# Expert routing in two halves of the tokens, with the first product and silu of two tiles computed during the routing

## The chip, the cores and the metric

The kernel runs on one core of one Trainium2 chip. The metric is the device time of one execution in microseconds, and the number quoted is the median of several executions. The profile shows one further execution of the same program: for each engine its instructions with start and duration, and what released it after each idle stretch.

## The reference

A small image and text model of one block. Thirty-two images pass through a Fourier operator of four layers and become 64 tokens of width 64 each; 77 text tokens are appended to each image, so there are 32 * 141 = 4512 tokens. An attention follows, and then a mixture of experts, which is all that the change touches:

```
h = h + ffn(layernorm(h))
logits   = x @ gate_w + gate_b                 # 16 experts
probs    = softmax(logits)
top-2 of probs, divided by their sum           -> dispatch[token, expert], zero elsewhere
h1 = x @ w1[e]; h2 = x @ w2[e]                 # 64 -> 128, for every expert
hidden = silu(h1) * h2
out = sum over e of dispatch[token, e] * (hidden @ w3[e])     # 128 -> 64
```

Every expert is computed for every token, and the shares of the two chosen experts weigh the results. All numbers are float32.

## The kernel before, in words

The program is a chain of blocks with a barrier of all engines between them: the Fourier operator and its head, the attention, and `build_moe` (L1379 on). Every engine's list of instructions is written out by hand, and engines are ordered by semaphores alone; each engine works through its list in order, so an instruction that waits holds all that stand behind it on that engine. SyncE (SP) issues all transfers.

In the expert block the 4512 tokens stand on 96 partitions with 47 tokens each. A tile is 4 such columns, 384 tokens; there are 12 tiles, the last with 288. Each tile has 8 steps, each for a pair of experts, one on partitions 0 to 63 and the other on 64 to 127; so there are 96 steps, s = 8 t + c.

The block begins with the layernorm (DVE and ACT, four chunks), 47 transposes of the tokens (L1486, into `xT`), and 94 small products for the logits (L1494). DVE adds the bias (L1631), subtracts the maximum (L1632, L1633), ACT takes the exponential (L1563), and DVE computes the shares of all 47 columns in a chain of 20 instructions (L1635 to L1652) in which each waits for the one before (`link`). PE transposes the shares (L1499); DVE and ACT copy one half of them each to `dTs` (L1654, L1565). SP stores them to `dT_d` in DRAM with six transfers (L1448), waits until all have landed, and then loads them back, spread over 64 partitions, into `dB` (L1457). One load group n is two transfers and serves four steps; `dB` holds two groups, so group n waits for GpSimd to be done with group n-2.

Then come the steps. For step s:

- PE computes h1 = w1 * xT (L1520), when the product of step s-2 is done;
- ACT takes its silu into `s1` (L1579);
- GpSimd (POOL) computes dx = xT * dB, tokens times share (L1475), into one of three buffers: it may be three steps ahead of PE;
- PE computes h2 = w2 * dx (L1527);
- DVE multiplies silu and h2 into `hid` (L1668).

h1 and h2 take turns in three pairs of PSUM banks, `HP2`. After 8 steps PE sums hid * w3 of the tile in `MA` (L1535, 16 matmul instructions, which the profile counts as 32), ACT copies the sum (L1571), PE folds the halves into `MO` (L1509), one tile late, and DVE adds them to `H` (L1659).

The wait of the main part on PE is of few lines:

```
for c in range(EP):
    s = t * EP + c
    if s >= 2:
        pe.wait_ge(S["prod"], s - 1)
    ...
    pe.wait_ge(S["dx"], s + 1)
    if s >= 1:
        pe.wait_ge(S["silu"], s)
    ...
```

Of the kernel before, what the change touches and what calls it, by code (L numbers as in the profile page):

```python
# [890 lines left out]
ROWS = 96  # L891
PER = TOK // ROWS
# [4 lines left out]
EXPERTS, HID = 16, 128  # L897
# [480 lines left out]
def build_moe(nc, H, out, dT_d, gate, gateb, w12, w3, aconst):  # L1378
# [3 lines left out]
    ALU, ACT, AX = mybir.AluOpType, mybir.ActivationFunctionType, mybir.AxisListType  # L1382
    ctx = ExitStack()
    with ctx:
        sb = lambda name, shape, dt=f32: ctx.enter_context(nc.sbuf_tensor(name, shape, dt))
        sem = lambda name: ctx.enter_context(nc.semaphore(name))
        TILE, EP = 4 * ROWS, EXPERTS // 2
# [3 lines left out]
        def js(t):  # L1391
            return min(4, PER - 4 * t)
# [11 lines left out]
        dB = sb("mdB", [128, 2, EP // 2, TILE])  # L1404
        dx = sb("mdx", [128, 3, TILE])
        s1 = sb("ms1", [128, 2, 2, TILE])
        hid = sb("mhid", [128, EP, 2, TILE])
        acc = sb("macc", [128, 2, TILE])
        stat = sb("mst", [96, 3 * PER + 1])
# [17 lines left out]
        def bank(i):  # L1427
            return HP2[i // 2][:, i % 2, :]
# [6 lines left out]
        @block.sync  # L1435
        def _(sp):
            sp.dma_start(cst[:, :], aconst[0:96]).then_inc(S["par"], 16)
            for e in range(2):
                r = slice(e * 64, e * 64 + 64)
                sp.dma_start(gs[r, :], gate).then_inc(S["par"], 16)  # L1440
                sp.dma_start(w1s[r], w12.rearrange("d (c e) m -> e d c m", e=2)[e]).then_inc(S["par"], 16)
                sp.dma_start(fold[r, :], aconst[0:64, PER + 128 + EXPERTS:PER + 128 + EXPERTS + 64]).then_inc(S["par"], 16)
            sp.dma_start(w3s[:, :, :], w3).then_inc(S["par"], 16)
            sp.dma_start(gb[:, :], gateb.broadcast_to([96, EXPERTS])).then_inc(S["par"], 16)
            sp.wait_ge(S["dte"], 2)
            for g in range(6):
                k = min(8, PER - 8 * g)
                sp.dma_start(dT_d.rearrange("e (j p) -> j e p", p=96)[8 * g:8 * g + k], dTs[0:16 * k, g, :]).then_inc(S["dst"], 16)  # L1448
            sp.wait_ge(S["dst"], 96)
            d_v = dT_d.rearrange("(c e) n -> e c n", e=2)  # L1450
            for n in range(2 * TILES):
                t, c, k = n // 2, n % 2 * 4, js(n // 2) * 96
                if n >= 2:
                    sp.wait_ge(S["dx"], 4 * (n - 1))
                for e in range(2):
                    src = d_v[e, c:c + 4, t * TILE:t * TILE + k].rearrange("(o c) n -> o c n", o=1).broadcast_to([64, 4, k])
                    sp.dma_start(dB[e * 64:e * 64 + 64, n % 2, :, 0:k], src).then_inc(dbs[n % 2], 16)  # L1457
                if n % 2 == 1 and t >= 2:
                    store_tile(sp, t - 2)
            for t in range(TILES - 2, TILES):  # L1460
                store_tile(sp, t)
            sp.wait_ge(S["st"], 16 * TILES)
# [15 lines left out]
        def _(pe):  # L1478
# [14 lines left out]
                    if j < PER:  # L1493
                        last = nc.tensor.matmul(bank(4 + e)[0:96, i * 16:i * 16 + 16], xT[r, j * 96:j * 96 + 96], gs[r, :], start=True, stop=True)  # L1494
            last.then_inc(S["lg"], 1)
            pe.wait_ge(S["rt"], 1)
            for g in range(6):
                k = 16 * min(8, PER - 8 * g)
                last = nc.tensor.matmul(bank(g // 3)[0:k, g % 3 * 96:g % 3 * 96 + 96], disp[:, g * 128:g * 128 + k], ident[:, 0:96], start=True, stop=True, is_transpose=True)  # L1499
                if g % 3 == 2:  # L1500
                    last.then_inc(S["dt"], 1)
            pe.wait_ge(S["dte"], 2)

            def output(t):
                pe.wait_ge(S["accd"], t + 1)
# [6 lines left out]
            for t in range(TILES):  # L1512
                k = js(t) * 96
                for c in range(EP):
                    s = t * EP + c
                    if s >= 2:
                        pe.wait_ge(S["prod"], s - 1)
                    for e in range(2):
                        r = slice(e * 64, e * 64 + 64)
                        last = nc.tensor.matmul(HP2[2 * s % 3][:, e, 0:k], w1s[r, c, 0:HID], xT[r, t * TILE:t * TILE + k], start=True, stop=True)  # L1520
                    last.then_inc(S["h1"], 1)
                    pe.wait_ge(S["dx"], s + 1)
                    if s >= 1:
                        pe.wait_ge(S["silu"], s)
                    for e in range(2):
                        r = slice(e * 64, e * 64 + 64)
                        last = nc.tensor.matmul(HP2[(2 * s + 1) % 3][:, e, 0:k], w1s[r, c, HID:2 * HID], dx[r, s % 3, 0:k], start=True, stop=True)  # L1527
                    last.then_inc(S["h2"], 1)

                if t:  # L1530
                    pe.wait_ge(S["accd"], t)
                for c in range(EP):
                    pe.wait_ge(S["prod"], t * EP + c + 1)
                    for e in range(2):
                        last = nc.tensor.matmul(MA[e * 64:e * 64 + 64, 0:k], w3s[:, 2 * c + e, :], hid[:, c, e, 0:k], start=c == 0, stop=c == EP - 1)  # L1535
                    last.then_inc(S["acc"], 1)
                if t:
                    output(t - 1)
# [3 lines left out]
        def _(act):  # L1542
# [18 lines left out]
            act.wait_ge(S["lgd"], 1)  # L1561
            lg = scr[:, 0:PER * EXPERTS]
            nc.scalar.activation(lg, lg, ACT.Exp).then_inc(S["lgd"], 1)  # L1563
            act.wait_ge(S["dt"], 2)
            nc.scalar.activation(dTs[:, 3:6, :], bank(1)[:, 0:288].rearrange("p (g n) -> p g n", n=96), ACT.Copy).then_inc(S["dte"], 1)  # L1565

            def whole(t):
                act.wait_ge(S["acc"], (t + 1) * EP)
# [4 lines left out]
            for s in range(STEPS):  # L1573
                t, c = s // EP, s % EP
                k = js(t) * 96
                act.wait_ge(S["h1"], s + 1)
                if s >= 2:
                    act.wait_ge(S["prod"], s - 1)
                nc.scalar.activation(s1[:, s % 2, :, 0:k], HP2[2 * s % 3][:, :, 0:k], ACT.Silu).then_inc(S["silu"], 1)  # L1579
                if c == 1 and t:  # L1580
                    whole(t - 1)
            whole(TILES - 1)
# [2 lines left out]
        def _(dve):  # L1585
            chained = [0]

            def link(ins):
                chained[0] += 1
                ins.then_inc(S["chain"], 1)  # L1590
                dve.wait_ge(S["chain"], chained[0])
# [31 lines left out]
            def over_e(x):  # L1623
                return x.rearrange("p (j o) -> p j o", o=1).broadcast_to([ROWS, PER, E_])

            def over_j(x, k=PER):
                return x.rearrange("p (o e) -> p o e", o=1).broadcast_to([ROWS, k, E_])
# [4 lines left out]
            link(nc.vector.tensor_reduce(cols[0], lg, axis=AX.X, op=ALU.max))  # L1632
            nc.vector.tensor_tensor(lg, lg, over_e(cols[0]), ALU.subtract).then_inc(S["lgd"], 1)  # L1633
            dve.wait_ge(S["lgd"], 2)
            link(nc.vector.tensor_reduce(cols[0], lg, axis=AX.X, op=ALU.add))  # L1635
            link(nc.vector.reciprocal(cols[0], cols[0]))
            link(nc.vector.tensor_tensor(pr, lg, over_e(cols[0]), ALU.mult))
            link(nc.vector.tensor_copy(rest, pr))
            for top, one in ((cols[1], one1), (cols[2], one2)):
                link(nc.vector.tensor_reduce(top, rest, axis=AX.X, op=ALU.max))  # L1640
                link(nc.vector.tensor_tensor(hit, rest, over_e(top), ALU.is_equal))  # L1641

                link(nc.vector.scalar_tensor_tensor(idx, hit, -float(E_), over_j(order), ALU.mult, ALU.add))  # L1643
                link(nc.vector.tensor_reduce(cols[3], idx, axis=AX.X, op=ALU.min))
                link(nc.vector.tensor_tensor(one, idx, over_e(cols[3]), ALU.is_equal))
                if one is one1:
                    link(nc.vector.scalar_tensor_tensor(rest, one, -2.0, rest, ALU.mult, ALU.add))
            link(nc.vector.tensor_tensor(cols[1], cols[1], cols[2], ALU.add))
            link(nc.vector.reciprocal(cols[1], cols[1]))
            link(nc.vector.tensor_tensor(one1, one1, one2, ALU.add))  # L1650
            link(nc.vector.tensor_tensor(pr, pr, one1, ALU.mult))
            nc.vector.tensor_tensor(disp.rearrange("p (j e) -> p j e", e=E_), pr, over_e(cols[1]), ALU.mult).then_inc(S["rt"], 1)  # L1652
            dve.wait_ge(S["dt"], 1)
            nc.vector.tensor_copy(dTs[:, 0:3, :], bank(0)[:, 0:288].rearrange("p (g n) -> p g n", n=96)).then_inc(S["dte"], 1)  # L1654

            def finish(t):
                dve.wait_ge(S["ot"], t + 1)
# [3 lines left out]
            for s in range(STEPS):  # L1661
                t, c = s // EP, s % EP
                k = js(t) * 96
                dve.wait_ge(S["h2"], s + 1)
                dve.wait_ge(S["silu"], s + 1)
                if s >= EP:
                    dve.wait_ge(S["acc"], s - EP + 1)
                nc.vector.tensor_tensor(hid[:, c, :, 0:k], HP2[(2 * s + 1) % 3][:, :, 0:k], s1[:, s % 2, :, 0:k], ALU.mult).then_inc(S["prod"], 1)  # L1668
                if c == 1 and t >= 2:
                    finish(t - 2)  # L1670
            finish(TILES - 2)
# [64 lines left out]
```

## Time and profile before

| | us |
|---|---|
| median of 3 runs | 2551.52 |
| lowest and highest | 2549.45, 2554.74 |
| the profiled execution's own time | 2540.21 |
| its span | 2538.4 |
| PE busy | 2173.8 (86%) |
| ACT busy | 1667.6 (66%) |
| DVE busy | 1648.9 (65%) |
| POOL busy | 152.2 (6%) |
| mean granted clock of TensorE | 0.937 of full |

The span goes from the first to the last instruction seen; the execution's own time has 1.8 us around it. The expert block is the last 278 us of the span: it starts at 2261 us. In rows of the timeline the first number is the start, the second the duration, then engine, line, operation, output <- inputs, shapes and count; in brackets stands the idle time before it and what ended it. PE's instructions are float32 products, which the profile shows as two entries each. The granted clock is 1.00 at 2.4 GHz and 0.50 at 1.2 GHz.

### The profile page before, as it was taken

To read this page: it belongs to the slowest core of one execution; us is meant where nothing else is said; L and a number is where in the kernel's file an instruction comes from. 1 tells how busy PE (TensorE), PEld (TensorE's weight loads), DVE (VectorE), ACT (ScalarE), POOL (GpSimd) and SP (SyncE) were. 2 spreads that over 40 slices of the span, in tenths; PEclk is the share of its full clock that TensorE was granted. 3 is DMA by queue.
4 is the path that set the end of the run, shared out by engine and by line. 5 is a ranking of instruction groups with operands and counts; after the bars stand their busy time and mean duration, and the time that the engine had idled before them with its cause. 6 is when DMAs were issued, how large, how long until landed. Compare 5 with 4: busy or idle time off the path is not lost. (4 is left out here: it accounts for less than half of the span.)

```text
span 2538.4 us, 79362 instructions
## 1 busy us (share of the span) xinstructions
PE 2173.8 (86%) x34571; PEld 1444.8 (57%) x34571; DVE 1648.9 (65%) x2562; ACT 1667.6 (66%) x2640; POOL 152.2 (6%) x172
## 2 busy tenths in 40 slices
PE   7779989976997998599979966996999599964999
PEld 4657757755665776566657755664222355552444
DVE  4868878884777887577778884776000576754444
ACT  1924468875776787767778875775999466641433
POOL 0000000000000000000000000000000022201443
PEclk9989989998999999899989998998999699976999
DMA  5656657658996873899957658997653100012433
GB/s 184 227 179 240 235 209 264 211 186 267 370 372 230 293 263 137 267 319 377 367 215 263 210 197 278 363 375 283 231 178 95 36 2 2 2 28 55 105 84 74
DMA packets 175734, 524.91 MB, mean 207 GB/s; under 512 B 22879, under 2 KB 37951, under 8 KB 175167
## 3 DMA queue, kind: packets, MB, share of 16 engines
q1 hardware_dynamic: 175391, 519.84, 60.1%
q8 instruction: 276, 4.52, 0.7%
q14 instruction: 67, 0.55, 0.1%
HBM read 350.02 MB, written 170.37 MB: 205 GB/s over the span
## 5 line engine op out<-in xcount | busy, mean ns | idle before, releaser
L416 PE MATMUL P<-cst,mem 128*128 128x128 f32 (+1 forms) x3760 | 502.2, 283 | 53.0 <-ACT mem L709 13.9
L675 ACT ACTIVATE mem<-P,small 128x512 f32<-128x512 f32 x512 | 309.8, 688 | 310.1 <-PE P L524 249.3
L416 PEld LDWEIGHTS P<-cst,mem 128*128 128x128 f32 (+1 forms) x3760 | 415.9, 144 | 161.5 <-issue 126.2
L832 DVE BATCH_NORM_STATS2 mem<-mem 128x6 f32<-128x512 f32 x512 | 315.2, 678 | 5.7 <-ACT mem L675 5.7
L870 DVE COPY mem<-P 128x512 f32<-128x512 f32 x384 | 248.0, 686 | 99.8 <-PE P L416 98.4
L524 PEld LDWEIGHTS P<-cst,mem 64*128 64x128 f32 (+1 forms) x5120 | 239.2, 166 | 95.9 <-issue 95.7
L524 PE MATMUL P<-cst,mem 64*128 64x128 f32 (+1 forms) x5120 | 260.4, 275 | 0.0
L665 ACT ACTIVATE mem<-mem,small 128x1024 f32<-128x1024 f32 x192 | 229.1, 1250 | 39.4 <-DMA mem<-z_d 39.4
L825 DVE COPY mem<-P 128x512 f32<-128x512 f32 x256 | 165.0, 686 | 127.5 <-PE P L501 127.5
L820 DVE COPY mem<-P 128x512 f32<-128x512 f32 x256 | 165.4, 686 | 119.9 <-PE P L416 119.9
L709 ACT ACTIVATE mem<-mem,small 128x1024 f32<-128x1024 f32 x192 | 232.8, 1248 | 6.3 <-DMA mem<-z_d 5.3
L501 PE MATMUL P<-cst,mem 64*64 64x64 f32 x8192 | 164.5, 230 | 63.9 <-DMA mem<-G_d 40.6
L514 PE MATMUL P<-mem,wbd 64*64 64x512 f32 x1536 | 195.1, 605 | 20.5 <-ACT mem L675 18.2
L470 PE MATMUL P<-mem 128*64 128x64 f32 x4096 | 142.1, 232 | 69.5 <-DVE mem L801 37.9
L501 PEld LDWEIGHTS P<-cst,mem 64*64 64x64 f32 x8192 | 143.8, 142 | 88.3 <-issue 71.4
L470 PEld LDWEIGHTS P<-mem 128*64 128x64 f32 x4096 | 135.3, 146 | 77.8 <-issue 48.0
L1668 DVE TENSOR_TENSOR mhid<-MH,ms 128x768 f32<-128x768 f32 (+1 forms) x96 | 90.3, 941 | 124.3 <-ACT ms L1579 104.2
L1579 ACT ACTIVATE ms<-MH 128x768 f32<-128x768 f32 (+1 forms) x96 | 76.5, 797 | 134.7 <-PE MH L1520 134.7
L1270 ACT ACTIVATE AP<-AP,anm 128x141 f32<-128x141 f32 x320 | 112.8, 356 | 57.9 <-DVE anm L1355 57.7
L717 ACT ACTIVATE mem<-P 128x512 f32<-128x512 f32 x192 | 104.2, 594 | 68.7 <-PE P L600 67.9
L1017 PE MATMUL HP<-hz,hf 64*128 64x512 f32 x512 | 133.9, 635 | 15.3 <-ACT hz L985 14.7
L992 ACT ACTIVATE hg<-HP,hb 128x1024 f32<-128x1024 f32 x128 | 144.1, 1492 | 1.9 <-PE HP L1017 1.9
(164 smaller groups left out, 2936.3 us busy)
## 6 DMA issues: line engine op xcount, KB each, us to landing
mem<-z_d SPq DMA_DIRECT2D x360, 512.0 KB, 5.1
z_d<-mem SPq DMA_DIRECT2D x256, 512.0 KB, 6.9
mem<-in_wmix SPq DMA_DIRECT2D x64, 1024.0 KB, 8.6
G_d<-mem SPq DMA_DIRECT2D x128, 256.0 KB, 4.0
mem<-G_d SPq DMA_DIRECT2D x128, 256.0 KB, 7.6
hz<-z_d SPq DMA_DIRECT2D x64, 512.0 KB, 4.3
mdB<-dT_d SPq DMA_DIRECT2D x44, 384.0 KB, 5.7
mem<-in_x SPq DMA_DIRECT2D x128, 12.0 KB
```

The costliest lines, as they stand in the source:

```text
L416: return nc.tensor.matmul(out, in_, ident[0:n, 0:n], start=True, stop=True, is_transpose=True)
L470: last = nc.tensor.matmul(P[n % 8][x * 64:x * 64 + 64, i * 64:i * 64 + 64], SG[s % 3][:, o:o + 64], mem[:, k:k + 64], start=True, stop=True)
L501: last = nc.tensor.matmul(P[v][w * 64:w * 64 + 64, m * 64:m * 64 + 64], Gt[a.par][o, x:x + 64], i1c[o, k:k + 64], start=True, stop=True)
L514: nc.tensor.matmul(P[4 + 2 * (a.q % 2) + x][w * 64:w * 64 + 64, :], pw[o, o], zbuf[a.par][o, n:n + 512], start=True, stop=False)
L524: last = nc.tensor.matmul(P[4 + 2 * (a.q % 2) + x][w * 64:w * 64 + n, j * 128:j * 128 + 128], ATs[o, a.q % 2, c:c + n], i2c[o, x * 128:x * ...
L665: nc.scalar.activation(z, z, ACT.Gelu, bias=bbi, scale=bsc).then_inc(S["z_gelu_c"], 1)
L675: nc.scalar.activation(ychunk(l, a, h), P[4 + 2 * (a.q % 2) + h][:, :], ACT.Identity, bias=bias0 if first else pwb_c).then_inc(S["eY"], 1)
L709: nc.scalar.activation(zq[a.s % FR], src, ACT.Gelu, bias=bbi, scale=bsc).then_inc(S["z_gelu"], 1)
L820: nc.vector.tensor_copy(ATs[:, a.q % 2, :], P[2 + a.q % 2][:, :]).then_inc(S["eT3"], 1)
L825: nc.vector.tensor_copy(Ai[a.par].rearrange("p (y h z k) -> p h y z k", h=2, z=2, k=2 * KX)[:, b, :, :, v * KX:v * KX + KX], P[v][:, :].re ...
L832: nc.vector.bn_stats(so, ychunk(l, a, h)).then_inc(S["eS"], 1)
L870: nc.vector.tensor_copy(hTq[a.s % 2][:, h * 512:h * 512 + 512], P[h][:, :]).then_inc(S["eT1"], 1)
```

## The change

The shares are computed, transposed, copied and stored in two halves: columns 0 to 23 (tiles 0 to 5), then columns 24 to 46. SP starts to load `dB` when the first half has landed. The bias, maximum and exponential are still taken for all columns at once. The first product h1 and its silu of steps 0 to 15 (tiles 0 and 1) move ahead: PE starts them when the maximum has been subtracted, eight before the first half of the transposes and eight after it. Their silus go to a new buffer `s1a`, of 16 steps, so that PE's h1 for them leaves the main loop and so does ACT's silu. The transposes go to `MA` and `MO` in place of the banks of `HP2`; ACT copies both halves.

SP:

```diff
-            sp.wait_ge(S["dte"], 2)
-            for g in range(6):
-                k = min(8, PER - 8 * g)
-                sp.dma_start(dT_d.rearrange("e (j p) -> j e p", p=96)[8 * g:8 * g + k], dTs[0:16 * k, g, :]).then_inc(S["dst"], 16)
-            sp.wait_ge(S["dst"], 96)
+            def store_shares(half):
+                sp.wait_ge(S["dte"], half + 1)
+                for g in range(3 * half, 3 * half + 3):
+                    k = min(8, PER - 8 * g)
+                    sp.dma_start(dT_d.rearrange("e (j p) -> j e p", p=96)[8 * g:8 * g + k], dTs[0:16 * k, g, :]).then_inc(S["dst"], 16)
+            store_shares(0)
+            sp.wait_ge(S["dst"], 48)
             for n in range(2 * TILES):
+                if n == 2:
+                    store_shares(1)
+                if t == TILES // 2:
+                    sp.wait_ge(S["dst"], 96)
                 if n >= 2:
                     sp.wait_ge(S["dx"], 4 * (n - 1))
```

PE:

```diff
-            pe.wait_ge(S["rt"], 1)
-            for g in range(6):
...
+            def shares(half):
+                pe.wait_ge(S["rt"], half + 1)
+                for g in range(3 * half, 3 * half + 3):
+                    k = 16 * min(8, PER - 8 * g)
+                    last = nc.tensor.matmul((MA, MO)[half][0:k, g % 3 * 96:g % 3 * 96 + 96], disp[:, g * 128:g * 128 + k], ident[:, 0:96], start=True, stop=True, is_transpose=True)
+                last.then_inc(S["dt"], 1)
+            pe.wait_ge(S["lgd"], 1)
+            for s in range(AHEAD):
+                t, c = s // EP, s % EP
+                if s >= 3:
+                    pe.wait_ge(S["silu"], s - 2)
+                for e in range(2):
+                    r = slice(e * 64, e * 64 + 64)
+                    last = nc.tensor.matmul(HP2[s % 3][:, e, 0:TILE], w1s[r, c, 0:HID], xT[r, t * TILE:t * TILE + TILE], start=True, stop=True)
+                last.then_inc(S["h1"], 1)
+                if s == EP - 1:
+                    shares(0)
+            shares(1)
             pe.wait_ge(S["dte"], 2)
+            pe.wait_ge(S["silu"], AHEAD)
...
-                    for e in range(2):
-                        r = slice(e * 64, e * 64 + 64)
-                        last = nc.tensor.matmul(HP2[2 * s % 3][:, e, 0:k], w1s[r, c, 0:HID], xT[r, t * TILE:t * TILE + k], start=True, stop=True)
-                    last.then_inc(S["h1"], 1)
+                    if s >= AHEAD:
+                        for e in range(2):
+                            r = slice(e * 64, e * 64 + 64)
+                            last = nc.tensor.matmul(HP2[2 * s % 3][:, e, 0:k], w1s[r, c, 0:HID], xT[r, t * TILE:t * TILE + k], start=True, stop=True)
+                        last.then_inc(S["h1"], 1)
```

ACT:

```diff
-            act.wait_ge(S["dt"], 2)
-            nc.scalar.activation(dTs[:, 3:6, :], bank(1)[:, 0:288].rearrange("p (g n) -> p g n", n=96), ACT.Copy).then_inc(S["dte"], 1)
+            act.wait_ge(S["par"], 144)
+            for s in range(AHEAD):
+                act.wait_ge(S["h1"], s + 1)
+                nc.scalar.activation(s1a[:, s, :, :], HP2[s % 3][:, :, 0:TILE], ACT.Silu).then_inc(S["silu"], 1)
+                if s % EP == EP - 1:
+                    half = s // EP
+                    act.wait_ge(S["dt"], half + 1)
+                    if half:
+                        nc.scalar.activation(dTs[:, 3:5, :], MO[:, 0:192].rearrange("p (g n) -> p g n", n=96), ACT.Copy)
+                        nc.scalar.activation(dTs[0:112, 5, :], MO[0:112, 192:288], ACT.Copy).then_inc(S["dte"], 1)
+                    else:
+                        nc.scalar.activation(dTs[:, 0:3, :], MA[:, 0:288].rearrange("p (g n) -> p g n", n=96), ACT.Copy).then_inc(S["dte"], 1)
...
-                act.wait_ge(S["h1"], s + 1)
-                if s >= 2:
+                if s >= AHEAD:
+                    act.wait_ge(S["h1"], s + 1)
                     act.wait_ge(S["prod"], s - 1)
-                nc.scalar.activation(s1[:, s % 2, :, 0:k], HP2[2 * s % 3][:, :, 0:k], ACT.Silu).then_inc(S["silu"], 1)
+                    nc.scalar.activation(s1[:, s % 2, :, 0:k], HP2[2 * s % 3][:, :, 0:k], ACT.Silu).then_inc(S["silu"], 1)
```

DVE: the chain from L1635 to L1652 stands in a loop over `(0, 24), (24, PER)`, on these columns alone, each pass ending in `then_inc(S["rt"], 1)`; the copy of L1654 is gone; the product of step s reads `s1a[:, s]` for s < 16.

On PE, behind the logits, stood the transposes of the shares and then pairs of h1 (`MH<-mxT`) and h2 (`MH<-mdx`); `MH` is `HP2`, `mdisp` the shares:

```order
-L1494 MATMUL MH<-mg,mxT 96x16 x47
-L1499 MATMUL MH<-mc,mdisp 128x96 x5
-L1499 MATMUL MH<-mc,mdisp 112x96
-L1520 MATMUL MH<-mxT,mw 128x384 x2
-L1527 MATMUL MH<-mdx,mw 128x384 x2
-L1520 MATMUL MH<-mxT,mw 128x384 x2
-L1527 MATMUL MH<-mdx,mw 128x384 x2
```

Now the same place reads:

```order
+L1504 MATMUL MH<-mg,mxT 96x16 x47
+L1521 MATMUL MH<-mxT,mw 128x384 x16
+L1511 MATMUL MA<-mc,mdisp 128x96 x3
+L1521 MATMUL MH<-mxT,mw 128x384 x16
+L1511 MATMUL MO<-mc,mdisp 128x96 x2
+L1511 MATMUL MO<-mc,mdisp 112x96
+L1553 MATMUL MH<-mdx,mw 128x384 x16
+L1561 MATMUL MA<-mhid,mw 64x384 x16
```

Sixteen h1 (two instructions each) now stand between the logits and the first h2, eight ahead of each half of the transposes, and the eight steps of a tile before the sum (`MA<-mhid`) are h2 alone.

On SP, in the same place of the program, the change makes of six stores (`dT_d<-mdT`) ahead of the first load:

```order
+L1453 DMA dT_d<-mdT 8x16x96 [waits m_dte]
+L1453 DMA dT_d<-mdT 8x16x96 x2
+L1467 DMA mdB<-dT_d 64x4x384 [waits m_dst]
+L1467 DMA mdB<-dT_d 64x4x384 x3
+L1453 DMA dT_d<-mdT 8x16x96 [waits m_dte]
+L1453 DMA dT_d<-mdT 8x16x96
+L1453 DMA dT_d<-mdT 7x16x96
+L1467 DMA mdB<-dT_d 64x4x384 [waits m_dx]
```

Three stores stand ahead of the first two load groups, and three between them and group 2; the wait of the latter for `m_dte` is new.

On ACT, from the exponential (`mscr<-mscr`) on:

```order
+L1589 ACTIVATE mscr<-mscr 96x752 [waits m_lgd]
+L1593 ACT_TABLE_LOAD [waits m_h1]
+L1593 ACTIVATE ms1a<-MH 128x768 [waits m_par]
+L1593 ACTIVATE ms1a<-MH 128x768 [waits m_h1] x7
+L1601 ACTIVATE mdT<-MA 128x288 [waits m_dt]
+L1593 ACTIVATE ms1a<-MH 128x768 [waits m_h1] x8
+L1598 ACTIVATE mdT<-MO 128x192 [waits m_dt]
+L1599 ACTIVATE mdT<-MO 112x96
```

Each copy of a half of the shares (`mdT<-`) stands behind eight silus, and the load of the function table for silu stands behind the exponential with a wait for the first h1.

## Rows read from the trace of the kernel before

**Rows 1.** The page: the chain that ended last, by line
```profile
PE MH L1520 3%; PE MH L1527 2%; PE MA L1535 2%; PE MO L1509 0%; PE MH L1494 0%; DMA mdB<-dT_d 0%; PE MH L1486 0%; DVE mst L1604 0%; DVE mst L1598 0%; SPq L1448 0%; DMA dT_d<-mdT 0%; DVE mxn L1611 0%; DVE mxn L1600 0%; DVE mscr L1643 0%; DVE mscr L1641 0%
```

**Rows 2.** Windows: PE, PEld, DVE, ACT, POOL busy; granted clock; DMA share, GB/s
```profile
2293.45:2304.95 11.50, 0.00 (x0) 0.00 (x0) 10.26 (x12) 0.83 (x1) 0.00 (x0) 0.50 0.00 0
2325.60:2328.60 3.00, 1.90 (x6) 1.19 (x8) 0.20 (x1) 0.00 (x0) 2.95 (x4) 0.50 0.73 139
2326.70:2331.70 5.00, 5.00 (x16) 2.88 (x18) 1.70 (x2) 0.81 (x1) 3.43 (x4) 0.50 0.30 62
2331.70:2345.15 13.45, 13.37 (x80) 5.88 (x76) 5.96 (x7) 4.86 (x6) 6.47 (x7) 0.99 0.50 108
2345.15:2362.69 17.54, 17.47 (x106) 8.40 (x106) 7.66 (x8) 6.86 (x9) 8.10 (x8) 1.00 0.41 91
```

**Rows 3.** Timeline, from the bias to the end of the shares' chain
```profile
2290.36 1.12 DVE L1631 TENSOR_TENSOR mscr<-MH,mgb 96x384 f32<-96x384 f32 x2 [8.42 <-PE MH L1494]
...
2293.45 0.83 ACT L1563 ACTIVATE mscr<-mscr 96x752 f32<-96x752 f32 x1 [9.88 <-DVE mscr L1633]
...
2294.32 0.93 DVE L1635 TENSOR_REDUCE msm<-mscr 96x47 f32<-96x752 f32 x1 [0.90 <-ACT mscr L1563]
2295.28 0.45 DVE L1636 RECIPROCAL msm<-msm 96x47 f32<-96x47 f32 x1
...
2296.73 0.55 DVE L1638 COPY mscr<-mscr 96x752 f32<-96x752 f32 x1
...
2310.65 0.94 DVE L1652 TENSOR_TENSOR mdisp<-mscr,msm 96x752 f32<-96x752 f32 x1
```

**Rows 4.** The chain of waits, from the copied shares to h2: start, duration, what
```profile
2312.91 0.42 ACT mdT L1565
...
2313.34 0.68 SPq L1448
...
2316.55 2.26 DMA dT_d<-mdT
...
2319.50 5.99 DMA mdB<-dT_d
...
2326.70 1.65 PE MH L1527 x4
```

**Rows 5.** Timeline of the same place: DVE's copy, h1 and its silu
```profile
2312.43 0.46 DVE L1654 COPY mdT<-MH 128x288 f32<-128x288 f32 x1 [0.84 <-PE MH L1499]
...
2313.37 1.65 PE L1520 MATMUL MH<-mxT,mw 64*128 64x384 f32 x4 [0.50 <-ACT mdT L1565]
2315.07 0.81 ACT L1579 ACTIVATE ms<-MH 128x768 f32<-128x768 f32 x1 [0.45 <-PE MH L1520]
```

**Rows 6.** The chain of waits in tiles 0 and 1
```profile
2328.35 1.28 PE MH L1520 x4
...
2332.77 0.65 PE MH L1520 x4
...
2334.10 0.92 PE MH L1520 x4
...
2339.84 5.31 PE MA L1535 x32
...
2356.56 1.76 PE MA L1535 x9
```

**Rows 7.** Timeline in tile 0: product and dx side by side
```profile
2334.15 1.02 POOL L1475 TENSOR_TENSOR mdx<-mxT,mdB 128x384 f32<-128x384 f32 x1 [0.28 <-PE MH L1527]
2334.37 0.96 DVE L1668 TENSOR_TENSOR mhid<-MH,ms 128x768 f32<-128x768 f32 x1 [0.33 <-ACT ms L1579]
```

**Rows 8.** Timeline in the attention: DVE with POOL running, and without
```profile
2205.64 3.27 POOL L1133 TENSOR_TENSOR aQK<-aQ,aK 128x423 f32<-128x423 f32 x3 [8.43 <-DVE aK L1346]
...
2205.99 1.20 DVE L1370 TENSOR_TENSOR aV<-aE,aV 128x423 f32<-128x423 f32 x1
...
2209.38 0.59 DVE L1370 TENSOR_TENSOR aV<-aE,aV 128x423 f32<-128x423 f32 x1
```

More of the change, by code:

```diff
@@ L1406, in build_moe @@
         s1 = sb("ms1", [128, 2, 2, TILE])
+        AHEAD = 2 * EP
+        s1a = sb("ms1a", [128, AHEAD, 2, TILE])
         hid = sb("mhid", [128, EP, 2, TILE])
@@ L1495, in _ @@
             last.then_inc(S["lg"], 1)
-            pe.wait_ge(S["rt"], 1)
-            for g in range(6):
[L1498 to L1501, printed above, removed]
+            def shares(half):
[16 more added lines that the diff above has]
+            shares(1)
             pe.wait_ge(S["dte"], 2)
+            pe.wait_ge(S["silu"], AHEAD)
             def output(t):
@@ L1634, in _ @@
             dve.wait_ge(S["lgd"], 2)
[L1635 to L1654, printed above, removed]
+            for lo, hi in ((0, 24), (24, PER)):
+                n = hi - lo
+                over = lambda x: x[:, lo:hi].rearrange("p (j o) -> p j o", o=1).broadcast_to([ROWS, n, E_])
+                lg_, pr_, hit_, idx_, one1_, one2_, rest_ = (x[:, lo:hi] for x in arr)
+                c0, c1, c2, c3 = (x[:, lo:hi] for x in cols)
+                link(nc.vector.tensor_reduce(c0, lg_, axis=AX.X, op=ALU.add))
+                link(nc.vector.reciprocal(c0, c0))
+                link(nc.vector.tensor_tensor(pr_, lg_, over(cols[0]), ALU.mult))
+                link(nc.vector.tensor_copy(rest_, pr_))
+                for top, one in ((1, one1_), (2, one2_)):
+                    link(nc.vector.tensor_reduce(cols[top][:, lo:hi], rest_, axis=AX.X, op=ALU.max))
+                    link(nc.vector.tensor_tensor(hit_, rest_, over(cols[top]), ALU.is_equal))
+                    link(nc.vector.scalar_tensor_tensor(idx_, hit_, -float(E_), over_j(order, n), ALU.mult, ALU.add))
+                    link(nc.vector.tensor_reduce(c3, idx_, axis=AX.X, op=ALU.min))
+                    link(nc.vector.tensor_tensor(one, idx_, over(cols[3]), ALU.is_equal))
+                    if top == 1:
+                        link(nc.vector.scalar_tensor_tensor(rest_, one, -2.0, rest_, ALU.mult, ALU.add))
+                link(nc.vector.tensor_tensor(c1, c1, c2, ALU.add))
+                link(nc.vector.reciprocal(c1, c1))
+                link(nc.vector.tensor_tensor(one1_, one1_, one2_, ALU.add))
+                link(nc.vector.tensor_tensor(pr_, pr_, one1_, ALU.mult))
+                nc.vector.tensor_tensor(disp.rearrange("p (j e) -> p j e", e=E_)[:, lo:hi], pr_, over(cols[1]), ALU.mult).then_inc(S["rt"], 1)
@@ L1667, in _ @@
                     dve.wait_ge(S["acc"], s - EP + 1)
-                nc.vector.tensor_tensor(hid[:, c, :, 0:k], HP2[(2 * s + 1) % 3][:, :, 0:k], s1[:, s % 2, :, 0:k], ALU.mult).then_inc(S["prod"], 1)
+                nc.vector.tensor_tensor(hid[:, c, :, 0:k], HP2[(2 * s + 1) % 3][:, :, 0:k], (s1a[:, s] if s < AHEAD else s1[:, s % 2])[:, :, 0:k], ALU.mult).then_inc(S["prod"], 1)
                 if c == 1 and t >= 2:
```

## The prediction

> **What bounds the kernel now.** I went from the page to the windows, then to the timeline and the chain of waits in the expert block, the only part that changes. The page's chain names the lines of `build_moe` first: h1, h2 and the sum on PE, then the loads of `mdB` and the shares' lines on DVE [rows 1]. The reader should see two different bounds in the windows [rows 2]. From 2345.15 to 2362.69, a tile in steady state, PE is busy 17.47 of 17.54 us at the full clock: PE sets the pace, and DVE, ACT and POOL have some 8 us of work each. Before 2326.7 nothing of that holds: from 2293.45 to 2304.95 PE has no work at all, while DVE works through the shares. The shares' chain runs on DVE from 2294.32 to 2311.59, 17.3 us [rows 3]. Then the shares travel: the last copy ends at 2313.33, six stores are issued from 2313.34 to 2317.2 and have landed at 2318.81, the first load group lands at 2325.5, POOL makes the first dx, and h2 of step 0 starts at 2326.70 [rows 4]. So h2(0) stands 15.1 us behind the end of the shares' chain, and of it PE had work for the six transposes and the 1.65 us of h1(0) alone [rows 5].
>
> **Term 1: when the first half of the shares is ready.** Sixteen of the 20 DVE instructions cover all elements (0.93 to 0.94 us, 0.97 with the gap behind each), one is the copy (0.55), two are reciprocals (0.45), and the rest of the 17.3 us, 17.3 - 15.5 - 0.6 - 0.95 = 0.25, is the short addition [rows 3]. The half size stands in the trace: the bias takes 1.12 for one instruction of 384 and one of 368 elements, 0.58 each with gap. A half is then 16 * 0.58 = 9.3, the copy 0.4 (between 0.28, half of it, and 0.55), the reciprocals 0.33 each (between half and whole of 0.45, gap included), the addition 0.25: 10.6 us. First half ready at 2304.9, 6.7 us earlier than all were; second at 2315.5, 3.9 later than all were.
>
> **Term 2: from there to h2(0).** Before, 15.1 us. Three stores fewer: the six starts span 2316.55 - 2313.34 = 3.2, so 0.64 each, 1.9 less. Three transposes and one copy less: before, the second copy ended 1.7 behind the shares; now the first three transposes (DVE's copy began 0.84 behind the last share) and one copy of 0.42 make 1.3, 0.4 less [rows 4, 5]. The landing of a store (2.26) and of the first load group (issue 0.6, landing 5.99 behind the second issue) I keep. So h2(0) starts at 2304.9 + 15.1 - 2.3 = 2317.7 in place of 2326.70: **9.0 us**.
>
> Three things could be later than 2317.7. PE's first eight h1: from 2293.5 at the half clock, a full set of four matmul entries takes 1.65 alone and 1.28 in a row [rows 5, 6], so 8 * 1.28 + 0.37 = 10.6, end at 2304.1, 0.8 before the shares are there. ACT: table load and first silu wait for h1(0); I read a silu at 0.81 [rows 5], shorter than 1.28, so ACT follows PE and its copy is not late. The second round: eight more from 2305.6, at the half clock to 2316.2, silu to 2317.0, transposes meanwhile, two copies of some 0.5 in all: 2317.6, just in time. At the full clock it would be ACT's 0.85 that sets the pace, and all this ends 3 us earlier. On SP, the second three stores wait for this copy, and behind them waits load group 2, which must wait for POOL's step 3 anyway (about 2320.4): the stores are issued by 2319.6. Load group 1 follows group 0 at once: before, the two groups together kept the transfers going until 2328 or so [rows 2], 2.5 behind the landing of group 0, so now it lands at about 2319, ahead of POOL's step 4.
>
> **Term 3: tiles 0 and 1 without h1.** PE loses 16 * 0.65 = 10.4 us of work at the full clock [rows 6], but it can't have it all, since DVE becomes the bound. h2(s) waits for the product of s-2; that chain is 0.05 + h2 alone 0.92 + 0.05 + product 0.96, 1.98 for two steps, and a product at 0.96 plus gap and dx at 1.02 [rows 7] give the same: 1.0 us a step instead of 1.44. From the first h2 to the sum: 7 * 1.0 + 0.92 = 7.9 us. Before it was 11.4 in tile 1 (2345.15 to 2356.56) and 13.1 in tile 0 (2326.70 to 2339.84) [rows 2, 4, 6], the latter because its first 5 us ran at a granted clock of 0.50. Will tile 0 start at the half clock again? PE has run h1 shortly before, but stands still for some 2 us twice; I take half clock for the first four steps. Those then cost 1.35 each (0.05 + 1.65 + 0.05 + 0.96 for two steps), 1.4 more: 9.3. The sums (5.31 a tile) stay. Gain 13.1 - 9.3 + 11.4 - 7.9 = **7.3 us**; bounds are 0 (step pace unchanged) and 10.4 plus the 2.6 that the half clock costs now, 13.0.
>
> **At nothing:** ACT's own pace (it has eight spare us per tile), the eight-bank swap to `MA`/`MO` (both empty then), the wait for all stores at tile 6 (80 us later), tiles 2 to 11, whose order is unchanged. Load groups 2 and 3 would be needed at about 2332 and 2336 and can be issued at 2320.4 and 2324.6, some 6.6 us before landing: the cover is the sum of tile 0.
>
> **Sum.** 9.0 + 7.3 = 16.3 us off the profiled execution's 2540.21, 2523.9. That execution lay 11.3 below the median; I carry the difference over to the median: 2551.52 - 16.3 = **2535.2**.
>
> **The rivals.**
> (a) *POOL and DVE get in each other's way.* In tiles 0 and 1 both now run with hardly a gap. In the attention a DVE product took 1.20 beside a running POOL and 0.59 without [rows 8]. If products and dx excluded each other here, a step would cost 0.96 + 1.02 = 1.98: 16 * 0.98 = 15.7 lost, gain 0.6, 2550.9. Against: product and dx do overlap in the trace at 0.96 and 1.02 [rows 7], the product having one operand in PSUM, that of the attention both in SBUF. The Trainium skill, GPSIMD Engine Reference, section Specifications, has GpSimd share its SBUF interfaces with VectorE, in contention with DVE instructions of two SBUF inputs; by that rule the 1.20 is expected and the product here is spared, and the trace agrees. Taken without its condition, it would give this rival.
> (b) *The steps don't shorten,* because POOL's loads or the waits hold them at 1.44: gain 9.0, 2542.5.
> (c) *The run ahead is late,* so the change does not start the main part when it says: if h1 steps don't overlap (1.65 each), the first copy is 1.7 late and the second ends 2 * 1.7 + 1.5 behind my 2317.6; gain some 11.5, 2540.
> (d) *Slower: TensorE's clock.* h2 alone fills 0.65 of each 1.0 us. If the granted clock stays at 0.50 through tiles 0 and 1 (11.0 for the steps, 10.6 for the sum, each), they take 43.2 instead of my 27.8, and the gain is 0.9. If it stays so for tile 2, another 17.5 is lost: 2568. The point from which it is over 0.2% slower is some 12 us of half clock in tile 2. For it: the clock was 0.50 through all of the routing, small matmuls included. Against: it rose 5 us behind h2(0), in work as dense as the sums here.
>
> **How the numbers follow.** About 5 us (0.2%) can be told from no change. The forecast 0.70 (with its neighbours up to 22 us of gain, both bounds of term 3 and the full clock), (b) 0.09, (c) 0.09, (a) 0.04, (d) half 0.04, (d) in full or something else slower 0.04. Faster 0.88, same 0.08, slower 0.04. The range reaches from 2551.5 - 22 = 2529, less 1 for the spread of runs, to case (b) plus the spread, 2545. Its own range for the forecast is 2531 to 2539.
>
> **What would show it.** Right: first dx near 2316.6; the first h2 near 2317.7; the second half's last share at 2315.5; h2 steps of 1.0 in tiles 0 and 1 with DVE's idle gone; tile 2 from 2346.3 in place of 2362.69. Wrong: the copy behind silu 7 later than the shares; products over 1.0 us (a); a granted clock of 0.50 past the first four steps (d); POOL waiting for `mdB` at steps 4, 8 or 12 (b).

## The result and the profile after

| | before | after |
|---|---|---|
| median of 4 runs | 2552.95 | 2532.81 |
| lowest and highest | 2549.45, 2554.74 | 2528.55, 2534.11 |
| the profiled execution's own time | 2540.21 | 2534.11 |
| its span | 2538.4 | 2532.3 |
| start of the exponential in the span | 2293.45 | 2303.82 |
| from there to the end of the span | 244.95 | 228.48 |

The ratio is 0.9923, 95% interval 0.9902 to 0.9945: 20 us faster, between 14 and 25. The medians lie 20.1 apart, the two profiled executions only 6.1. The table's last two rows say why the latter is no measure of the change: the exponential, which stands behind everything that was left alone but ahead of everything that was moved, started 10.4 us later in the second execution. I therefore count from the start of the exponential. There the change gives 244.95 - 228.48 = **16.5 us**. The kernel before has one run more here than ahead of the prediction, which puts its median at 2552.95 in place of 2551.52.

Windows of the changed kernel, with the columns of [rows 2] (the first line names them): the first run of h1 in two pieces, PE's wait for the first half of the shares, the start of the second run of h1, PE's wait for the second half, the steps of tile 0 in two pieces, and the steps of tile 1.

```profile
core 0: us, PE busy (x) PEld busy (x) DVE busy (x) ACT busy (x) POOL busy (x), PEclk, DMA share, GB/s
2303.82:2307.20 3.38, 3.36 (x10) 1.86 (x12) 2.35 (x6) 2.44 (x3) 0.00 (x0) 0.50 0.00 0
2307.20:2311.63 4.43, 4.43 (x24) 2.02 (x20) 4.19 (x8) 4.42 (x7) 0.00 (x0) 0.84 0.00 0
2311.63:2315.37 3.74, 0.00 (x0) 0.00 (x0) 3.50 (x9) 1.09 (x2) 0.00 (x0) 1.00 0.00 0
2316.00:2319.00 3.00, 3.00 (x11) 1.73 (x12) 2.79 (x7) 1.22 (x2) 0.00 (x0) 0.53 0.13 33
2322.90:2325.60 2.70, 0.00 (x0) 0.00 (x0) 2.52 (x6) 1.14 (x2) 0.00 (x0) 1.00 1.09 227
2328.00:2331.98 3.98, 3.98 (x12) 1.66 (x13) 1.92 (x2) 0.00 (x0) 3.63 (x4) 0.50 0.39 75
2331.98:2337.10 5.12, 4.63 (x23) 1.71 (x21) 4.40 (x5) 0.00 (x0) 3.08 (x4) 0.95 0.71 157
2342.40:2350.05 7.65, 6.84 (x35) 2.50 (x33) 6.22 (x7) 0.49 (x1) 4.96 (x5) 1.00 0.52 105
```

Where [rows 2] had no PE work at all between the exponential and the shares, PE now works and DVE has no gap. The granted clock rises during the first run of h1 and is still 1.00 while PE stands still for 3.7 and for 2.7 us. It is down again when PE has work again: 0.53 at the start of the second run of h1, 0.50 when h2 begins. From the middle of tile 0 on it is 1.00.

The timeline from the exponential to the first dx, answering to [rows 3] and [rows 5]:

```profile
2303.82 0.83 ACT L1589 ACTIVATE mscr<-mscr 96x752 f32<-96x752 f32 x1 [9.88 <-DVE mscr L1669]
...
2303.84 7.79 PE L1521 MATMUL MH<-mxT,mw 64*128 64x384 f32 x32 [3.23 <-DVE mscr L1669]
...
2304.68 0.55 DVE L1676 TENSOR_REDUCE msm<-mscr 96x24 f32<-96x384 f32 x1 [0.90 <-ACT mscr L1589]
...
2306.88 5.85 ACT L1593 ACTIVATE ms1a<-MH 128x768 f32<-128x768 f32 x8
...
2314.77 0.55 DVE L1693 TENSOR_TENSOR mdisp<-mscr,msm 96x384 f32<-96x384 f32 x1
...
2315.38 0.74 PE L1511 MATMUL MA<-mc,mdisp 96*128 96x96 f32 x3 [3.75 <-DVE mdisp L1693]
...
2316.16 0.41 ACT L1601 ACTIVATE mdT<-MA 128x288 f32<-128x288 f32 x1 [3.43 <-PE MA L1511]
...
2325.65 0.74 PE L1511 MATMUL MO<-mc,mdisp 96*128 96x96 f32 x3 [2.75 <-DVE mdisp L1693]
2326.42 0.33 ACT L1598 ACTIVATE mdT<-MO 128x192 f32<-128x192 f32 x1 [2.38 <-PE MO L1511]
...
2326.86 3.87 POOL L1485 TENSOR_TENSOR mdx<-mxT,mdB 128x384 f32<-128x384 f32 x4 [77.73 <-DMA mdB<-dT_d]
```

The first half of the chain takes 10.6 us (2304.68 to 2315.32), the second ends at 2325.59, 20.9 us behind the start. PE waits 3.75 us with its first eight h1 done; eight silus take 5.85, 0.73 each, so ACT is done before it too.

The chain of waits from the stores' landing to tile 2, answering to [rows 4] and [rows 6]:

```profile
2317.96 2.00 DMA dT_d<-mdT
...
2320.65 6.05 DMA mdB<-dT_d
...
2328.00 4.38 PE MH L1553 x12
...
2337.17 5.31 PE MA L1561 x32
...
2343.37 0.97 DVE mhid L1707
...
2344.38 0.94 PE MH L1553 x4
...
2345.35 0.97 DVE mhid L1707
...
2348.34 1.78 PE MH L1553 x8
2350.12 5.31 PE MA L1561 x32
2355.43 0.82 PE MO L1534 x8
```

In tile 1 h2 and product alternate: 0.97 of DVE, 0.04, 0.94 of PE, 0.02, then DVE again. That is the chain of two steps that the prediction priced at 1.98; here it takes 2345.35 - 2343.37 = 1.98.

Counted from the exponential, in us (before, after): first h2 33.25, 24.18; sum of tile 0 46.32, 33.28; first h2 or h1 of tile 1 51.63, 38.59; its sum 63.04, 46.23; tile 2 69.17, 52.36.

### The profile page after: what moved, and what is told of

Same layout as the page of the kernel before. It is cut to its first block and busy times, and to the rows that moved or that the text cites. A ratio compares the mean times of both kernels' runs of the same rounds, so it can differ in the third digit from the quotient of the medians.

```text
span 2532.3 us, 79373 instructions
## 1 busy us (share of the span) xinstructions
PE 2178.8 (86%) x34571; PEld 1442.3 (57%) x34571; DVE 1651.5 (65%) x2581; ACT 1668.9 (66%) x2642; POOL 151.7 (6%) x172
## 5 line engine op out<-in xcount | busy, mean ns | idle before, releaser
L675 ACT ACTIVATE mem<-P,small 128x512 f32<-128x512 f32 x512 | 310.2, 688 | 320.5 <-PE P L524 259.1
L1031 DVE TENSOR_SCALAR hob<-HO,hb 128x512 f32<-128x512 f32 x16 | 12.0, 751 | 196.3 <-PE HO L1006 196.3
L646 ACT ACTIVATE mem<-mem 64x1024 f32<-64x1024 f32 x64 | 137.1, 2154 | 2.2 <-DVEq L257 0.6
```

What stands on the lines that cost most here:

```text
L675: nc.scalar.activation(ychunk(l, a, h), P[4 + 2 * (a.q % 2) + h][:, :], ACT.Identity, bias=bias0 if first else pwb_c).then_inc(S["eY"], 1)
```

## The experiments

Each is compared by the same marks, counted in us from the start of the exponential, since the execution as a whole moves by more than most of the differences. The marks are those of one profiled execution; two executions of one program had their end within 0.2 us of each other (244.95 and 244.76 before the change, 228.48 and 228.43 behind it). Where five or more runs were made, the ratio to the kernel before is given too; the third bank, the extra matmuls, the two other cuts and rival (a) were run once.

### Each part alone

Halves only: no h1 and no silu ahead.

```diff
-        AHEAD = 2 * EP
+        AHEAD = 0
```

> Only the two halves of the shares are kept; no h1 or silu is done ahead, all 96 steps are as in the kernel before. Counted from the start of the exponential, the kernel before has its first h2 at 33.25 us and the end of the span at 244.95; the changed kernel has 24.2 and 228.5. Theory (the two parts add up: 9.0 us from the earlier load, 7.4 from the shorter tiles 0 and 1): first h2 at 24.2, end at 236, so 9 us faster than the kernel before, ratio 0.9965. Rival (the early start is worth less, because the second half of the shares' chain keeps DVE until 21 us and the half clock lasts longer): end at 239 or more, 6 us or less.

Measured: first h2 at 24.55, end at 235.91, that is 9.0 us gained. Ratio 0.9943 (0.9924 to 0.9961).

Run ahead only: all 16 h1, then the shares in one piece; six stores, then the loads.

```diff
-            for lo, hi in ((0, 24), (24, PER)):
+            for lo, hi in ((0, PER),):
...
-                if n == 2:
-                    store_shares(1)
...
-                if s == EP - 1:
-                    shares(0)
+            shares(0)
             shares(1)
```

> Only the run ahead is kept: h1 and silu of 16 steps during the routing, while the shares are computed, stored and loaded in one piece as in the kernel before. Theory (additive): first h2 within 0.5 us of 33.2, tiles 0 and 1 shorter by 7.4, end of the span at 237.5 from the exponential, 7.4 us faster than the kernel before, ratio 0.997. Rival (without h1 in the loop the loads of the shares hold the steps, so the two tiles gain little by themselves): end at 242 or more.

Measured: first h2 at 32.84, end at 237.14: 7.8 us gained, ratio 0.9962 (0.9950 to 0.9975). The steps of tile 0 take 42.28 - 32.84 = 9.4, those of tile 1 7.63. Together 16.8, against 16.5 for both at once. The parts add up, and the rivals named for the two runs (an end at 239 or more, at 242 or more) fall.

### The pace of a tile without h1

```diff
-                    if s >= 2:
-                        pe.wait_ge(S["prod"], s - 1)
+                    if s >= AHEAD or s >= 3:
+                        pe.wait_ge(S["prod"], s - 1 if s >= AHEAD else s - 2)
```

> The changed kernel, but in tiles 0 and 1 h2 waits for the product three steps back, not two (the banks allow it while no h1 is between). If the chain of h2, 0.92, and product, 0.96, per two steps sets the pace of 0.99 a step, the step falls to DVE's own 0.91 to 0.96 and tile 1's steps take 7.3 in place of 7.64 us. If DVE or POOL alone sets it, nothing changes: 7.6.

Measured: tile 1's steps take 6.84 (from 37.39 to 44.23), tile 0's 8.17, and the end comes at 226.47, 2.0 earlier than in the changed kernel. Tile 1 in the timelines of DVE and of POOL:

```profile
2336.68 7.01 DVE L1707 TENSOR_TENSOR mhid<-MH,ms1a 128x768 f32<-128x768 f32 x8 [4.86 <-PE MH L1553]
```

```profile
2336.73 4.88 POOL L1485 TENSOR_TENSOR mdx<-mxT,mdB 128x384 f32<-128x384 f32 x5 [2.34 <-PE MH L1553]
```

So the alternation was the bound, not an engine. With it gone, DVE has no gap within the tile and its own 0.88 a product sets the pace. A product that follows another at once costs 7.01 / 8 = 0.88, less than the 0.96 of one alone, which is why it went below my 7.3.

### The clock at the first h2

```diff
+            for i in range(8):
+                nc.tensor.matmul(MO[:, 0:TILE], w1s[0:64, 0, 0:HID], xT[0:64, 0:TILE], start=True, stop=True)
             shares(1)
             pe.wait_ge(S["dte"], 2)
             pe.wait_ge(S["silu"], AHEAD)
+            for i in range(4):
...
```

> The changed kernel with twelve more matmuls of 384 columns on PE, whose results nobody reads, eight before the second half of the transposes and four behind it, so that PE doesn't stand still before the first h2. Theory (tile 0's steps take 9.10 us where tile 1's take 7.64 because the granted clock is 0.50 at the first h2): with the clock at 1.00 there, tile 0's steps take 7.6 to 7.9 and the end comes 1.2 to 1.5 us earlier than in the changed kernel, 227.1 from the exponential. Rival (tile 0's steps are long because its loads and dx arrive late): they still take 9.0 or more at a clock of 1.00.

Measured: first h2 only at 29.07, end at 233.52. It doesn't answer the question. The extra matmuls used one half of PE's rows and so cost some 0.66 each, as much as a pair of h1 (0.65), and pushed the transposes from 21.83 to 25.36; and the clock was not held:

```profile
2323.98:2328.98 5.00, 4.58 (x14) 2.56 (x15) 1.37 (x2) 0.00 (x0) 1.33 (x2) 0.68 0.08 19
2328.98:2333.98 5.00, 4.61 (x24) 1.51 (x20) 4.54 (x6) 0.00 (x0) 3.64 (x4) 1.00 0.71 156
```

The second try had pairs on both halves of the rows, into `MA` and `MO`:

```diff
+            def idle(n):
+                for i in range(n):
+                    for e in range(2):
+                        r = slice(e * 64, e * 64 + 64)
+                        nc.tensor.matmul((MA, MO)[e][:, 0:TILE], w1s[r, 0, 0:HID], xT[r, 0:TILE], start=True, stop=True)
+            pe.wait_ge(S["dte"], 1)
+            idle(4)
             shares(1)
...
+            idle(2)
```

> The first try with extra matmuls pushed the second half of the transposes 3.5 us back. Now the changed kernel with six pairs of extra matmuls, each pair side by side on the two halves of PE's rows like h1, four pairs before the second half of the transposes and two behind it; their results are read by nobody. Theory: the first h2 stays at 24.2 to 24.6, the clock is 1.00 there, tile 0's steps take 7.6 to 7.9 in place of 9.10. Rival: they take 9.0 or more with the clock at 1.00.

Measured: first h2 at 25.44, later than I wanted (the transposes came 1.2 late), but at a clock of 1.00, and the steps of tile 0 then take 32.98 - 25.44 = 7.54, as in tile 1. End at 228.17. Windows from the first h2 on, and DVE:

```profile
2322.63:2326.43 3.80, 3.38 (x20) 1.61 (x20) 1.70 (x2) 0.00 (x0) 3.31 (x4) 1.00 0.35 74
2326.43:2331.43 5.00, 4.61 (x24) 1.53 (x22) 4.54 (x6) 0.00 (x0) 3.28 (x4) 1.00 0.72 166
```

```profile
2324.73 1.82 DVE L1715 TENSOR_TENSOR mhid<-MH,ms1a 128x768 f32<-128x768 f32 x2 [4.54 <-PE MH L1561]
2326.71 1.82 DVE L1715 TENSOR_TENSOR mhid<-MH,ms1a 128x768 f32<-128x768 f32 x2 [0.15 <-PE MH L1561]
```

So the half clock costs 9.10 - 7.54 = 1.6 us in tile 0. One thing besides the clock differs: with h2 1.3 us later, POOL is further ahead of it. The run with the cut behind column 16 (below) separates the two. There the first h2 also comes at 25.44, with all three dx ready, but at the half clock, which lasts some 3 us:

```profile
2324.00:2326.00 2.00, 2.00 (x6) 1.18 (x8) 0.30 (x1) 0.00 (x0) 0.26 (x1) 0.50 0.13 30
```

Its steps of tile 0 take 34.23 - 25.44 = 8.79. So 1.25 us of clock are left where dx is no question, and the rival (late loads and dx) falls as the main cause.

### Rival (a): DVE and POOL side by side

```diff
-                nc.vector.tensor_tensor(hid[:, c, :, 0:k], HP2[(2 * s + 1) % 3][:, :, 0:k], (s1a[:, s] if s < AHEAD else s1[:, s % 2])[:, :, 0:k], ALU.mult).then_inc(S["prod"], 1)
+                nc.vector.tensor_tensor(hid[:, c, :, 0:k], HP2[(2 * s + 1) % 3][:, :, 0:k] if s >= AHEAD else s1a[:, (s + 1) % AHEAD, :, 0:k], (s1a[:, s] if s < AHEAD else s1[:, s % 2])[:, :, 0:k], ALU.mult).then_inc(S["prod"], 1)
```

> The changed kernel, but in tiles 0 and 1 DVE multiplies two silus from SBUF with each other in place of silu and h2 from PSUM; this leaves h2 out of the result. It tests rival (a): DVE and POOL hinder each other when both inputs of DVE lie in SBUF, as in the attention (1.20 beside POOL, 0.59 without). Theory: products that run beside a dx take clearly more than the 0.87 to 0.96 us of the changed kernel, 1.5 or more, or dx takes more than 1.01; the steps of tile 1 take over 9 us in place of 7.64. If nothing changes (7.6), sharing isn't what stretched the instruction in the attention, and rival (a) was never possible.

Tile 1 in the timelines of DVE and of POOL:

```profile
2342.06 12.76 DVE L1707 TENSOR_TENSOR mhid<-ms1a 128x768 f32<-128x768 f32 x8 [3.80 <-PE MH L1553]
```

```profile
2342.10 13.58 POOL L1485 TENSOR_TENSOR mdx<-mxT,mdB 128x384 f32<-128x384 f32 x8 [2.97 <-PE MH L1553]
```

This version leaves h2 out of the result. Measured: products 12.76 / 8 = 1.6, dx 13.58 / 8 = 1.7, the steps of tile 1 11.25 (41.32 to 52.57), end at 234.83. The mechanism of the rival is real and strong; only the place of one operand keeps it away from the changed kernel. It isn't always DVE that pays. The first product of tile 0 started 0.04 us ahead of a dx and kept its 0.96; the dx took 1.79:

```profile
2325.49 0.96 DVE L1707 TENSOR_TENSOR mhid<-ms1a 128x768 f32<-128x768 f32 x1 [3.95 <-PE MH L1553]
2325.53 1.79 POOL L1485 TENSOR_TENSOR mdx<-mxT,mdB 128x384 f32<-128x384 f32 x1
```

### The place of the cut

Behind column 16:

```diff
-            for lo, hi in ((0, 24), (24, PER)):
+            for lo, hi in ((0, 16), (16, PER)):
```

(The stores, transposes and copies go with it, in two and four groups.)

> The changed kernel with the shares cut behind column 16 in place of 24. Theory (the chain of the first part, then stores and load, sets the first h2): the first part is ready 2.3 us earlier and has one store less, but PE's eight h1 and ACT's eight silus then end at 9 us, behind the shares at 8.3, and the first h2 also waits for the second part, transposed and copied at about 22.3; so the first h2 comes at 22.3 to 22.6 in place of 24.18, and the end 1.5 to 2 us earlier, 226.7. If instead the landing of the loads is the bound whatever the cut, the first h2 stays at 24 and nothing is gained.

Measured: first h2 at 25.44, 1.3 later than in the changed kernel, end at 229.44. The first dx started at 19.5, 3.5 earlier, and ran into the second part of the shares' chain. DVE, then POOL:

```profile
2316.94 0.67 DVE L1687 TENSOR_TENSOR mscr<-mscr,msm 96x496 f32<-96x496 f32 x1
2317.64 0.19 DVE L1690 TENSOR_TENSOR msm<-msm 96x31 f32<-96x31 f32 x1
...
2318.25 1.34 DVE L1692 TENSOR_TENSOR mscr<-mscr 96x496 f32<-96x496 f32 x1
...
2321.03 1.37 DVE L1694 TENSOR_TENSOR mdisp<-mscr,msm 96x496 f32<-96x496 f32 x1
```

```profile
2318.07 3.80 POOL L1485 TENSOR_TENSOR mdx<-mxT,mdB 128x384 f32<-128x384 f32 x3 [74.23 <-DMA mdB<-dT_d]
```

The three last instructions of the chain take 1.34, 1.37 and 1.37 in place of 0.67 from the moment POOL starts; a dx takes 1.27. That is 2.1 us on the second part. My expected 22.3 was also too low by 1.1 without that, of which 0.9 is that I had counted the second part from the chain's start, not from the exponential.

Behind column 32, by the same edits:

> The changed kernel with the shares cut behind column 32. By the pace of the chain (0.72 an instruction of 512 elements) the first part is ready at 13.9 from the exponential in place of 11.5 and has one store more, 0.64; the second part is ready at 22.0. Theory: the first h2 at 24.2 + 2.4 + 0.6 = 27.2, the end at 231.5. With the cut behind 16 the first h2 came at 25.4, because dx and the shares' chain ran side by side and stretched each other; if so, 24 lies between the two costs. Rival (a later start has less of something else to pay, for instance DVE free earlier): first h2 at 25.5 or less.

Measured: first h2 at 27.30, end at 231.58. The pace of the chain explains this side to 0.1 us. The rival (25.5 or less) falls. Of the three cuts 24 is the best.

### More steps ahead

```diff
-        AHEAD = 2 * EP
-        s1a = sb("ms1a", [128, AHEAD, 2, TILE])
+        AHEAD = 3 * EP
+        s1a = sb("ms1a", [128, AHEAD - EP, 2, TILE])
+
+        def early(s):
+            return hid[:, s] if s < EP else s1a[:, s - EP]
...
-                if s == EP - 1:
+                if s == AHEAD // 2 - 1:
                     shares(0)
```

> The changed kernel with 24 steps ahead in place of 16, 12 before each half of the transposes; the silu of tile 0 is kept in hid and multiplied in place. Theory (PE and ACT have idle time of about 3.5 us before each half of the transposes, and DVE sets the pace of a tile without h1): tile 2 also takes 13.8 in place of 17.5 us, first h2 at 24.2 to 25.0, end of the span at 225 from the exponential, 3 to 4 us less than the changed kernel. Rival (ACT's silus make the copies of the shares late, and so the first load): first h2 at 27 or more, end at 228 or more.

Measured: first h2 at 24.09, end at 224.41: 4.1 less than the changed kernel, 20.5 less than before. Ratio 0.9911 (0.9898 to 0.9925). Tile 2 in the chain of waits shows h2 and product in turn, as in tile 1:

```profile
2351.47 0.95 DVE mhid L1710
...
2352.47 0.94 PE MH L1556 x4
...
2353.43 0.97 DVE mhid L1710
...
2354.45 1.78 PE MH L1556 x8
2356.23 5.31 PE MA L1564 x32
```

Both edits together, 24 steps ahead and the third bank:

> 24 steps ahead and h2 three products ahead of DVE, both edits together. If the gains add, tiles 1 and 2 take 6.9 for their steps, tile 0 8.0, and the end of the span comes at 224.4 - 0.9 - 0.8 - 0.9 = 221.8 from the exponential, 6.7 us less than the changed kernel and 23 less than the kernel before, ratio to before 0.991. Rival (POOL, whose dx take 0.98 each, or the loads of the shares, issued when POOL is done with a group, hold the faster tiles): end at 223 or more.

Measured: end at 221.59, 6.9 less than the changed kernel and 23.4 less than before; ratio 0.9916 (0.9893 to 0.9939), median 2526.09 beside 2546.14. Tile 1 again, PE, DVE and POOL:

```profile
2338.46 6.92 PE L1556 MATMUL MH<-mdx,mw 64*128 64x384 f32 x32
...
2339.43 6.14 DVE L1710 TENSOR_TENSOR mhid<-MH,ms1a 128x768 f32<-128x768 f32 x7 [4.93 <-PE MH L1556]
2339.47 4.90 POOL L1488 TENSOR_TENSOR mdx<-mxT,mdB 128x384 f32<-128x384 f32 x5 [1.84 <-PE MH L1556]
```

The gains add up, and the rival of POOL and the loads (an end at 223 or more) falls. By the marks this is the best of all versions; its ratio can't be told from that of 24 steps alone.

### The spread, and the changed kernel again

> The kernel before, against itself. It shows how far two sets of executions of one program lie apart: the ratio should be 1 within 0.002, and the time from the exponential to the end of the span 244.9 to 245.1, as in the first profile, while the stretch ahead of the exponential moves by up to 10 us.

The kernel before, unchanged. Measured: ratio 1.0009 (0.9992 to 1.0025), from the exponential to the end 244.76, but the exponential at 2307.44 in place of 2293.45. The last ACTIVATE of L675, in the Fourier layers, started at 1756.7 in the first profile and at 1770.6 in this one: 13.9 us of difference between two executions of the same program arise before that point.

> The changed kernel again, on the same chip and beside the same runs of the kernel before. If the 16.5 us inside the expert block are all that the change gives, the ratio comes out at 0.9935 and the rest of the 20 us of the first comparison was spread; if something else came with the change, the ratio stays near 0.992 and the exponential starts earlier than in the kernel before.

The changed kernel, unchanged. Measured: ratio 0.9941 (0.9925 to 0.9958), median 2535.19 beside 2550.74; first h2 at 24.08, end at 228.43. The exponential started at 2305.97, 1.5 us earlier than in the kernel before's profile of the same round, where in the first pair it had started 10.4 later; nothing ahead of the block goes with the change.

## Why the prediction was right

It said 2535.2 and 16.3 us less; the first comparison gave 2532.8 and 20.1 less, the second 15.6 less (medians), and the block itself 16.5 in the first pair of profiles and 244.76 - 228.43 = 16.3 in the second. The 3.8 us by which the first comparison goes beyond the prediction were not found again: the second has 0.9941, the predicted ratio was 0.9936, and 16.5 us lie within both intervals. What is left is of the size of the spread of the part ahead of the block, and 1.4 of it is the higher median of the kernel before. That the first comparison's 2532.8 lies so near to 2535.2 is in part luck; the 16.3 of the block is not.

By its steps:

- **Term 1.** A half of the chain in 10.6 us: measured 10.64. The second half at 21.2 behind the start: 20.9.
- **Term 2.** First h2 9.0 us earlier: 9.1, and 8.7 with the halves alone. The path from the first half of the shares to h2 was put at 12.8 and took 12.7, with the same landings as before (2.00 and 6.05 in place of 2.26 and 5.99).
- **The three things that could be late.** None was. The margin was larger than I had it: I had PE's first eight h1 end at 2304.1 on the old scale, 0.8 us ahead of the shares, since I left the clock at 0.50; it rose during the run, and PE waited 3.75. The second round, just in time by my account, was not late either: its copies ended at 2326.89, 1.1 us ahead of the first h2. For ACT I took 0.85 a silu; silus in a row take 0.73. Both errors are on the safe side, and they are the room into which 24 steps fit.
- **Term 3.** Tile 0's steps 9.10 (predicted 9.3), tile 1's 7.64 (7.9), together 7.7 gained at this place where I had 7.3. At the start of tile 2 the gain is 16.8, at the end of the span 16.5. Where the 0.3 goes stands below the list. I gave two reasons for the step of 1.0 us. The alternation of h2 and product is shown by the third bank (7.64 to 6.84). The other, that DVE's product with its gap and POOL's dx would give the same, was wrong: with the third bank they go on at 0.88 and 0.98. The assumed half clock at the first h2 is shown by the pairs of matmuls; I had priced it at 1.4, it cost 1.3 to 1.6.
- **Rival (a)**, 4 in 100. Right to be left aside, for the reason given: the product has one operand in PSUM. With both in SBUF a step costs 1.6 rather than my 1.98. But I looked for that contention at the product alone. Many instructions of the shares' chain have two inputs from SBUF, and what keeps it clear of POOL is 1.3 us between its end, 2325.59, and the first dx, 2326.86. An early cut loses by it. The rule of the Trainium skill, GPSIMD Engine Reference, section Specifications (contention with DVE instructions that have two SBUF inputs), fits all of this; in these runs it is a factor of 2.0 on the chain's instructions and 1.3 to 1.8 on dx.
- **Rival (b)**, loads or waits hold the steps at 1.44: the steps of tile 1 took 0.95, and POOL waited for `mdB` at neither step 4 nor step 12. At step 8 it did in the second profile, as at step 16 in both, but beside the sum on PE, and it was three steps ahead again before h2 went on. I had called a wait at step 8 a sign of this rival; it can stand there at no cost. **(c)**, the run ahead late: no. **(d)**, the clock at 0.50 through whole tiles: it was 0.50 for the first 4 us of tile 0 only.

The 0.3 us are lost in tile 7, one of the tiles that I had put at nothing: it takes 17.89 in both profiles of the changed kernel and with the halves alone, 17.54 in both profiles of the kernel before and with the run ahead alone. There DVE starts one product 0.43 us behind the silu that it needs:

```profile
2451.88 0.82 ACT ms L1615
...
2452.74 0.40 issue
2453.13 0.97 DVE mhid L1707
```

So the loss comes with the halves; its cause stays open.

## What to carry to other kernels

Before deciding how much work to move ahead of a serial chain, look at which engines stand still beside the chain and how long: here that was 17 us of PE, and 24 steps fitted where 16 were moved. When a stage loses a part of its work, look for the alternation of two engines through too few buffers, since that can set the pace while no engine is full. An early start of one engine can stretch the chain that another is still working on: check the operands' places of both before you cut a chain shorter.

## What the runs showed of the hardware

- Beside a running POOL a DVE instruction with two inputs in SBUF took twice its time when POOL had started first (0.67 to 1.37 for 496 elements), and POOL's took 1.27 to 1.79 in place of 0.98. The one that started 0.04 us ahead of POOL's kept its time (0.96). With one input in PSUM both keep it (0.96 and 1.01).
- Instructions in a row whose waits are met cost less than one alone: 0.88 and 0.96 for the product, 0.73 and 0.81 for the silu.
- Of two runs with extra matmuls around the second half of the transposes, the one with matmuls on one half of PE's rows had a clock of 1.00 up to 2322.40, 0.76 from there to 2325.05 and 0.50 to 2326.50, with PE busy all the while; the one with pairs on both halves kept 1.00. In both PE stood still for 0.56 us behind the transposes. What made the difference stays open: each was run once.
- Two executions of the same program differed by 14 us in their Fourier layers alone, and by 0.2 in the 245 us from the exponential to the end.
